# Expert results added to the residual rows by an accumulating scatter in DRAM

## The reference

```python
xn = layernorm(layernorm(x)) * gamma + beta
logits = xn @ Wr + br                       # 8 experts
top_vals, top_idx = top_k(logits, 2)
w = softmax(top_vals)
for e in range(8):
    y = y + (gelu(xn @ W1[e] + b1[e]) @ W2[e] + b2[e]) * w_full[..., e, None]
return x + y
```

## Time and profile before

| what | us |
|---|---|
| median of 3 runs | 8129.97 (8129.04 to 8130.97) |
| the profiled execution, its own time | 8128.7 |
| its span in the trace | 8126.9 |
| routing block, first to last instruction | 7078.5 to 7223.9 |
| experts, first gather to last scatter's issue | 7225.2 to 8010.6 |
| combine block, first load to the end | 8020.95 to 8126.9 |

### The profile page before, as it was taken

One profiled execution on the slowest core, in us unless ns is written; L12 is line 12 of the kernel. 1 busy time (PEld: TensorE's weight loads), 2 busy tenths in 40 slices (PEclk: granted clock), 3 DMA queues, 4 the chain that ended last, 5 costly groups with the idle time before them and its releaser, 6 DMA issues. The chain is left out here.

```text
span 8126.9 us, 152076 instructions
## 1 busy us (share of the span) xinstructions
PE 4740.2 (58%) x25092; PEld 3771.0 (46%) x25110; DVE 4678.9 (58%) x11632; ACT 1678.8 (21%) x7056; POOL 5035.3 (62%) x5320
## 2 busy tenths in 40 slices
PE   3444444444454666666656756565665556779994
PEld 3433333333343444444444544444444444559993
DVE  7722222222237777777777767777677777764445
ACT  3400000000022111111111431111111112563331
POOL 0177777777755777777777247777777774015552
PEclk9999999999997777877777787778787876869997
DMA  5411111111124555555555245555555553412226
GB/s 203 162 29 29 29 29 29 29 29 29 29 56 132 137 137 137 137 137 138 136 134 139 69 121 138 137 137 137 137 137 138 137 137 85 140 51 70 70 70 219
DMA packets 527200, 848.14 MB, mean 104 GB/s; under 512 B 147632, under 2 KB 373137, under 8 KB 519791
## 3 DMA queue, kind: packets, MB, share of 16 engines
q0 software_dynamic: 228576, 543.07, 26.7%
q1 hardware_dynamic: 265512, 274.99, 11.7%
q10 hardware_dynamic: 32358, 23.60, 0.9%
HBM read 750.78 MB, written 82.11 MB: 102 GB/s over the span
## 5 line engine op out<-in xcount | busy, mean ns | idle before, releaser
L769 POOL DMA_INDIRECT gat_rows<-gat_table,gat_idx x3278 | 3103.4, 947 | 1057.8 <-issue 944.7
L890 PE MATMUL gat_ps_sum<-gat_msg,gat_hot 128*128 128x260 f32 x6656 | 2267.8, 500 | 1263.5 <-DVE feat L909 1261.0
L890 PEld LDWEIGHTS gat_ps_sum<-gat_msg,gat_hot 128*128 128x128 f32 x6656 | 1562.4, 246 | 1605.0 <-DVE gat_msg L945 1150.5
L769 POOL DMA_INDIRECT gcn_rows<-gcn_table,gcn_idx x1614 | 1523.0, 944 | 787.4 <-issue 478.3
L890 PE MATMUL gcn_ps_sum<-gcn_rows,gcn_hot 128*128 128x64 f32 x3328 | 814.1, 426 | 1228.2 <-DMA gcn_rows<-gcn_table,gcn_idx 724.7
L890 PEld LDWEIGHTS gcn_ps_sum<-gcn_rows,gcn_hot 128*128 128x128 f32 x3328 | 741.1, 328 | 1301.2 <-DMA gcn_rows<-gcn_table,gcn_idx 658.3
L909 DVE SCALAR_TENSOR_TENSOR feat<-gcn_ps_sum,in_first,feat 128x64 f32 x416 | 118.0, 284 | 1572.2 <-PE gcn_ps_sum L890 1572.2
L873 PEld LDWEIGHTS gat_ps_near<-gat_tab,gat_hot_t 128*128 128x128 bf16 x6656 | 268.3, 101 | 766.4 <-issue 579.2
L945 DVE TENSOR_TENSOR gat_msg<-gat_rows,gat_ps_as 128x1024 f32<-128x1024 f32 x416 | 503.2, 1210 | 118.1 <-issue 117.4
L921 DVE TENSOR_TENSOR gat_hot<-gat_count,mod_t 128x512 f32<-128x512 f32 x832 | 566.4, 681 | 2.7
L873 PE MATMUL gat_ps_near<-gat_tab,gat_hot_t 128*128 128x24 bf16 x6656 | 309.8, 178 | 435.4 <-DVE gat_hot L921 431.3
(11 more groups left out here) (308 smaller groups left out, 6375.5 us busy)
## 6 DMA issues: line engine op xcount, KB each, us to landing
gat_mod<-mod_rows SPq DMA_DIRECT2D x832, 128.0 KB
gat_ahead<-gat_table SPq DMA_DIRECT2D x6400, 1.0 KB
gi_mods<-mod_rows SPq DMA_DIRECT2D x52, 1024.0 KB, 4.7
gat_rows<-gat_table,gat_idx POOLq DMA_INDIRECT x3278
gcn_ahead<-gcn_table SPq DMA_DIRECT2D x3200, 0.2 KB
gcn_ahead<-gcn_table ACTq DMA_DIRECT2D x3200, 0.2 KB
gcn_rows<-gcn_table,gcn_idx POOLq DMA_INDIRECT x1614, 2.4
gat_table<-feat SPq DMA_DIRECT2D x28, 910.0 KB, 5.3
```

Of the source, the lines that this page charges most:

```text
L769: pool.indirect_dma_start(B["rows"][:, j, k, :], None, table, bass.IndirectOffsetOnAxis(ap=B["idx"][:, j, k:k + 1], axis=0)).then_inc(rows ...
L890: mm = pe.matmul(B["ps_sum"][b][:, 0:width], B["hot"][:, j, k, :], rhs, start=(k == 0), stop=(k == CH - 1))
```

## The change

The sum of residual and expert results is now built in DRAM.

1. In the input block SyncE stores each finished quad of `feat` to a new DRAM tensor `sum_rows` (`keep`), one store of 512 KB per quad beside the load and the store of `z`.
2. In routing the two weights of each row go to a tile `pair`, and one DMA writes them behind the row's 256 features in `z_rows`, whose rows are now 258 elements long: 98 * 128 pieces of 8 bytes.
3. The gather of a slot brings a row's two weights with it. VectorE picks one of them by a mask (`choice`, worked out in routing: first or second choice) with one small multiply and one small reduce per slot, and after the bias it multiplies the 128x256 result by that weight.
4. The scatter adds to `sum_rows` in DRAM (`compute_op=ALU.add`). As a node's row now receives two additions, a scatter first waits until the scatter of the slot before has landed. Places without a node still have rows of their own.
5. The combine block is gone. In its place seven DMAs, four from SyncE's queue and three from ScalarE's, copy `sum_rows` to the output from DRAM to DRAM.

```diff
@@ build_ffn_input, SyncE
+                def keep(q):
+                    sp.wait_ge(taken, min(2 * q + 2, -(-NW // 2)))
+                    rows = sum_rows[four(q).start * P:four(q).stop * P, :].rearrange("(w p) f -> p w f", p=P)
+                    sp.dma_start(rows, feat[:, four(q), 0:FEAT]).then_inc(kept, 16)
-                turns(NQ, [(load, BQ + 2 + SLOTS), (store, 0)])
+                turns(NQ, [(load, BQ + 2 + SLOTS), (keep, BQ + 1), (store, 0)])
+                sp.wait_ge(kept, 16 * NQ)
@@ build_routing
-            link(dve.reciprocal(K["weight1"][:, :], gs[:, :]))
-            link(dve.tensor_tensor(K["weight2"][:, :], ge[:, :], K["weight1"][:, :], ALU.mult))
+            link(dve.reciprocal(pair[:, :, 0], gs[:, :]))
+            dve.tensor_tensor(pair[:, :, 1], ge[:, :], pair[:, :, 0], ALU.mult).then_inc(paired, 1)
...
+                sp.wait_ge(paired, 1)
+                    sp.dma_start(z_rows.rearrange("(w p) f -> p w f", p=P)[:, :, FEAT:FEAT + 2], pair[:, :, :]
+                                 ).then_inc(pair_out, 16)
+                sp.wait_ge(pair_out, 16)
...
+                dve.tensor_scalar(K["choice"][:, :, 0], block_f[:, :], float(NW), None, ALU.is_le)
+                dve.tensor_scalar(K["choice"][:, :, 1], block_f[:, :], float(NW), None, ALU.is_gt)
+                link(dve.tensor_tensor(token_f[:, :], row_f[:, :], second[:, :], ALU.subtract))
+                link(dve.tensor_tensor(row_f[:, :], token_f[:, :], gap_row[:, :], ALU.add))
@@ build_experts, GpSimd
                     wait(pool, turned, s - (RING - 1))
+                    wait(pool, picked, s - (RING - 1))
...
                     pool.wait_ge(placed, s + 1)
                     pool.wait_ge(rowed, s + 1)
+                    wait(pool, stored[(c - 1) % RING], 16 * (i + (c - 1) // RING + 1))
                     pool.sem_inc(begun, 1)
-                    pool.indirect_dma_start(y_rows, bass.IndirectOffsetOnAxis(ap=row[:, j:j + 1], axis=0),
-                                            y[:, j, :], None).then_inc(stored[j], 16)
+                    pool.indirect_dma_start(sum_rows, bass.IndirectOffsetOnAxis(ap=row[:, j:j + 1], axis=0),
+                                            y[:, j, :], None, compute_op=ALU.add).then_inc(stored[j], 16)
@@ build_experts, VectorE
                     dve.wait_ge(turned, s + 1)
+                    dve.tensor_tensor(part_w[:, c % RING, :], xg[:, c % RING, FEAT:FEAT + 2],
+                                      K["choice"][:, one(s), :].squeeze(1), ALU.mult).then_inc(picked, 1)
...
+                    dve.wait_ge(picked, s + 1)
+                    dve.tensor_reduce(weight[:, j:j + 1], part_w[:, j, :], AX, ALU.add).then_inc(summed, 1)
                     dve.wait_ge(down, s + 1)
                     wait(dve, stored[j], 16 * (i + c // RING))
                     dve.tensor_tensor(y[:, j, :], ps_y[b][:, 0:FEAT], b2b[:, bass.ds(e, 1), :].squeeze(1),
-                                      ALU.add).then_inc(placed, 1)
+                                      ALU.add).then_inc(biased, 1)
+                    dve.wait_ge(biased, s + 1)
+                    dve.wait_ge(summed, s + 1)
+                    dve.tensor_scalar(y[:, j, :], y[:, j, :], weight[:, j:j + 1], None, ALU.mult).then_inc(placed, 1)
@@ in place of build_combine
+def build_output(nc, M, K, S, sum_rows, out):
+    step = S.WB * P
...
+            for r in parts:
+                r1 = min(r + step, S.N)
+                eng.dma_start(out[r:r1, :], sum_rows[r:r1, :]).then_inc(written[b], 16)
```

More of the change, by code:

```diff
@@ L1584, in build_gnn, with build_ffn_input @@
         Mem.clear_signals(nc)
-def build_ffn_input(nc, M, K, S, x, Wr, br, z_rows):
+def build_ffn_input(nc, M, K, S, x, Wr, br, z_rows, sum_rows):
     N, NW, TAIL, EX = S.N, S.NW, S.TAIL, S.EX
@@ L1664, in store @@
                     sp.wait_ge(normed, q + 1)
-                    rows = z_rows[four(q).start * P:four(q).stop * P, :].rearrange("(w p) f -> p w f", p=P)
+                    rows = z_rows[four(q).start * P:four(q).stop * P, 0:FEAT].rearrange("(w p) f -> p w f", p=P)
                     sp.dma_start(rows, z[:, q % Z, 0:count(q), :]).then_inc(stored[q % Z], 16)
-                turns(NQ, [(load, BQ + 2 + SLOTS), (store, 0)])
+                def keep(q):
[4 more added lines that the diff above has]
+                sp.wait_ge(kept, 16 * NQ)
                 for j in range(Z):
@@ L1914, in _ @@
                                  W1[e].rearrange("(k p) h -> p k h", p=P)).then_inc(w1_in, 16)
+                sp.wait_ge(paired, 1)
+                with nc.allow_non_contiguous_dma(reason="a row's two weights behind its features"):
+                    sp.dma_start(z_rows.rearrange("(w p) f -> p w f", p=P)[:, :, FEAT:FEAT + 2], pair[:, :, :]
+                                 ).then_inc(pair_out, 16)
+                sp.wait_ge(pair_out, 16)
                 sp.wait_ge(w1_in, 16 * EX)
@@ L2054, in build_experts @@
          rowed, placed) = [M.sem("ffn_" + n) for n in names]
+        picked, summed, biased = [M.sem("ffn_" + n) for n in "picked summed biased".split()]
         gathered = [M.sem(f"ffn_gathered{j}") for j in range(RING)]
@@ new lines, in build_output, with copy, _ @@
+def build_output(nc, M, K, S, sum_rows, out):
+    written = [M.sem(f"out_written{b}") for b in range(2)]
+    step = S.WB * P
+    with nc.Block() as block:
+        def copy(eng, b):
+            parts = [r for r in range(0, S.N, step) if r // step % 2 == b]
+            for r in parts:
+                r1 = min(r + step, S.N)
+                eng.dma_start(out[r:r1, :], sum_rows[r:r1, :]).then_inc(written[b], 16)
+            eng.wait_ge(written[b], 16 * len(parts))
+        @block.sync
+        def _(sp):
+            copy(sp, 0)
+        @block.scalar
+        def _(act):
+            copy(act, 1)
@@ L2245, in build @@
     S = Shapes(x.shape[0], src.shape[0], Wr.shape[1], F1.shape[2])
-    z_rows = nc.dram_tensor("z_rows", (S.NW * P, FEAT), F32).ap()
-    y_rows = nc.dram_tensor("y_rows", ((2 * S.NW + S.NS) * P, FEAT), F32).ap()
+    z_rows = nc.dram_tensor("z_rows", (S.NW * P, FEAT + 2), F32).ap()
+    sum_rows = nc.dram_tensor("sum_rows", ((S.NW + S.NS) * P, FEAT), F32).ap()
     with ExitStack() as ctx:
@@ L2254, in build @@
         K["expert_of"] = M.sb("expert_of", [1, S.NS], I32)
-        for n in (1, 2):
-            K[f"weight{n}"] = M.sb(f"weight{n}", [P, S.NW])
+        K["choice"] = M.sb("choice", [P, S.NS, 2])
         assert S.EX <= WIDE - FEAT
         K["logits"] = K["feat"][:, 0:S.NW, FEAT:FEAT + S.EX]
-        build_ffn_input(nc, M, K, S, x, Wr, br, z_rows)
+        build_ffn_input(nc, M, K, S, x, Wr, br, z_rows, sum_rows)
         K["up_all"] = M.sb("up_all", [P, S.EX, 2 * S.HD + S.HD // P])
-        build_routing(nc, M, K, S, F1)
-        build_experts(nc, M, K, S, c1, F2, c2, z_rows, y_rows)
-        build_combine(nc, M, K, S, y_rows, out)
+        build_routing(nc, M, K, S, F1, z_rows)
+        build_experts(nc, M, K, S, c1, F2, c2, z_rows, sum_rows)
+        build_output(nc, M, K, S, sum_rows, out)
 _GNN = ["W_gcn", "b_gcn", "g0", "beta0", "W1", "a_src1", "a_dst1", "b1", "g1", "beta1", "W2", "a_src2", "a_dst2",
```

15 lines of the change are left out of this document (8 added, 7 removed).

## The result

| | before | after |
|---|---|---|
| median | 8129.67 us (8129.04 to 8130.97, 4 runs) | 8270.28 us (8270.23 to 8270.52, 4 runs) |
| span of the profiled execution | 8126.9 | 8268.5 |

The change makes the kernel slower: the ratio of after to before is 1.0172, with an interval of 1.0159 to 1.0185.

The account below looks back on a forecast made before the run. TensorE bound the experts block at 3.74 us a slot; the wait would make it 4.28. Terms +0.5 + 0.45 + 109.2 + 1.1 - 69.5 = +42 us on 8128.7 gave 8170.5, forecast 8172 us, range 8060 to 8380.

Parts of the forecast that it names:

- L: Experts block: landing time of an accumulating scatter, taken as 3.5 us; period 4.28 instead of 3.74 us, +109 us.
- The answer of GpSimd: Experts block: GpSimd's time from a landing to starting the next scatter, taken as 0.78 us per period.
- 8314 us with L = 4.2: Rival in the experts block: the addition is dear, period 4.98 us, +252 us; chance of a dear add 0.15.
- The copy: Output: 36.4 us at 382 GB/s replace 105.95, -69.5 us; rival at half rate 70 us, 0.10 together with two others.
- The wait is hidden: Rival in the experts block: scatters land within 2.96 us, TensorE stays the bound, 8062 us; chance 0.15.
- The add almost free: Rival in the experts block: only the second read costs, period 3.92 us, 8099 us; chance 0.21 with its neighbourhood.
- TensorE's clock falls: Rival in the experts block: one slot in eight at half clock, +86 us, 8258 us; 0.10 together with two others.
- The little pieces: Routing: the weights' DMA, taken as covered, 0 us; rival at 250 ns each +64 us, 0.10 together with two others.
- Input block: Input block: 25 more stores, 12.8 MB, raise transfers to some 294 GB/s and cost 0; 13 us without cover.
- Routing and VectorE: Routing's extra masks and link cost 0.5 us; VectorE's weighting delays the first scatter by 0.45 us, the period by 0.
- The last landing's 1.1 us: Gap between the last scatter and the next block: 10.35 us stay, plus 1.1 us for the longer landing.
- Signs: Expected in the profile after: scatters 4.28 us apart, GpSimd's scatter waiting for the DMA of `sum_rows`, TensorE's busy share 87%.

Follow-up runs that it names:

- experiment 2: Changed kernel, its scatter adding half of each row, adding 64 of 128 rows, or writing 64 rows plainly: 8173.62, 8125.34 and 8061.0 us.
- e1_plain_wait: Changed kernel with its wait kept, but the scatter only writes its rows and adds nothing: 8074.15 us.

## Why the prediction was wrong in size

The sign, the bound and the mechanism came as forecast, but the span grew by 141.6 us where the sum had 41.7. Of the 99.9 us between, 96 are one term.

- **The term that failed: L, the landing of an accumulating scatter, taken as 3.5 us.** It is 3.9, and the period L + 0.78 = 4.28 became 4.75: 203 x 0.473 = 96 us, of which L itself is 203 x 0.4 = 81. The 3.5 was the middle of two bounds, 2.8 and 4.2, given meaning afterwards as 0.4 for reading DRAM, 0.34 for bytes at 382 GB/s and 0.36 for descriptors. Measured against the plain scatter's 2.4, the run shows 0.60 us more for the issue and 0.9 behind it. The bytes were costed at the rate of the engines' long streams, 0.34 us for 131 KB, while by experiment 2 the addition takes each engine 0.83 us more than a plain write. The issue was given 0.36 us without a row for it. The upper bound of a gather and a scatter end to end, 4.2, lay nearer (0.3 off) than the value taken (0.4 off).
- The answer of GpSimd, 0.78, held: 0.80 in the chain. The last 0.05 us of the interval, 11 us in the sum, come from some late slots (14 intervals of over 5 us, where the median is 4.70).
- An error of 0.4 us in L is large in the sum only because the term is multiplied by 203. The working had this in its bounds (8314 us with L = 4.2), but put the likely value's own range at 3.37 to 3.9.
- *The copy.* 42.2 us against 36.4, +5.8. It runs at 303 GB/s, not 382: the combine block's mixed stream of loads and stores to and from SBUF was no price for DRAM to DRAM. Nor did the bytes count twice.
- *The wait is hidden:* right for a plain scatter (`e1_plain_wait`, 3 us in the block), wrong for this one. *The add almost free*, L = 3.14: the Trainium skill, "Collectives: The Full Stack", section "The bandwidth ceiling", has the add cost no cycles, only a second read. Here the addition takes 13.2 engine-us more than a plain scatter, where the gather of as many rows, the nearest thing to a read that the runs have, takes 7.3 to 7.9 in all. With L = 3.9 instead of 3.14, the measurement speaks against one second read as the whole price of adding rows of 1 KB. No run parts the reading from the adding, and the addition also goes in more packets.
- *TensorE's clock falls:* it did not. TensorE was busy for 804 of 965 us with pauses in each period, and the granted clock stayed 0.99.
- *The little pieces:* 19.5 us for 12,544 of them, 25 ns each per engine, where 87 ns had been taken. That row was misread: of q0's 25,631 packets half are under 512 bytes and the other half are of 2 KB (12,815 of them make the 26.30 MB), so 87 ns is the mean of two kinds and no price of a 256-byte packet. Cover was ample either way.
- *Input block:* the third stream cost nothing visible. The DMA rate rose from 196 to 291 GB/s, as worked out (294); the new stores land after 5.6 us and those of `z` after 7.0 instead of 5.2. The last store of `z` still starts 0.4 us earlier than before (7043.0 us), so the 1.3 us come behind it. The windows of the block's end are below: next to nothing is moved there, and PEclk is 0.57 instead of 0.68. One reading of the code was wrong: the queue waits in the store of `z` too (20.1 us in all before the change), not in the load alone.
- *Routing and VectorE:* no visible cost; the expected 0.5 and 0.45 us are not to be seen in blocks that came out 0.7 and 0.2 us shorter. The last landing's 1.1 us did not show either: the gap shrank by 0.35.
- *Signs:* GpSimd was to wait for the DMA of `sum_rows`, and did, but the group names ScalarE; only the chain shows it. TensorE's share came to 83% instead of 87.

The end of the input block, before and after:

```profile
7060.00:7078.50 18.50, 13.69 (x71) 11.13 (x71) 1.04 (x2) 3.91 (x6) 0.00 (x0) 0.68 0.01 1
7060.00:7079.80 19.80, 15.22 (x68) 12.42 (x67) 1.04 (x2) 3.91 (x6) 0.00 (x0) 0.57 0.00 1
```

## What to carry to other kernels

A wait that puts transfers one behind the other turns a latency into a period: compare landing time plus the engine's answer with the period of the bound, and when the landing isn't in any row, treat its error times the number of turns as the error of the forecast. Here, with a bound of 3.74 us, a chain of 3.2 us cost 3 us in all and one of 4.7 cost 203. When ordering is needed only between some pairs, arrange the work so that those stand two apart, which brought the experts' block from 965 us to 797, 30 of them spent on eight empty slots. And sums that live in DRAM may as well live in the output tensor.

A version that waits for the last scatter only where the expert changes would do without the empty slots and might save most of their 30 us. It wasn't tried.

## What the runs showed that was not expected

- An accumulating scatter goes as one packet per row, a plain one as one per four rows, and costs GpSimd 0.60 us more (1.59 against 0.99).
- Adding 128 rows of 1 KB takes the engines 19.1 engine-us in all, three times a plain scatter's 5.9, and the rows land 1.5 us later. Where a scatter need only wait for the one before the last, TensorE's period of 3.78 us comes back, at a DMA share of 0.45.
- A copy from DRAM to DRAM runs at 302 to 304 GB/s in 56 KB runs and in 1 KB rows alike, with the engines busy for 0.92 to 0.96 of it. Why an engine moves less here than between DRAM and SBUF stays open.
- 12,544 pieces of 8 bytes by one direct DMA land after 19.5 us, 25 ns for each piece of an engine, far less than the 87 ns that had been taken.
